# VectorE's preparations for a 3x3 convolution stage move from the attention stage's loop into the convolution stage, whose first band is reordered

## The reference, cut to what matters

```python
q, k, v = to_grid(conv1x1(x, Wq, bq)), to_grid(conv1x1(x, Wk, bk)), to_grid(conv1x1(x, Wv, bv))  # 8x8 pixel windows
attn = softmax(einsum('bgck,bgcl->bgkl', q, k) / sqrt(C))
x = x + from_grid(einsum('bgkl,bgcl->bgck', attn, v))
x = x + conv1x1(gelu(conv1x1(x, W1, b1)), W2, b2)
```

```python
enh = conv3x3_depthwise(conv1x1(x, w_conv1_pw, b_conv1_pw), w_conv1_dw, b_conv1_dw)
h1, h2 = split(conv3x3_grouped(x, w_conv2_g, b_conv2_g))
attn = conv1x1(h1 * h2, w_conv2_pw) * attgamma + conv1x1(x, w_conv211)      # 16 coefficients for each pixel
attk = einsum('bpn,nm->bpm', attn, selfw)                                   # kernels: 2 inputs x 9 taps for each output
x2 = einsum('bpgij,bpgj->bpgi', attk, patches(enh)) + einsum('bpn,nc->bpc', attn, selfb)
x = x2 * ga1 + enh + x
```

## Time and profile before

| | before |
|---|---|
| median of 3 runs | 5592.44 us (5592.13 to 5592.62) |
| the profiled execution | 5592.69 us, its span 5591.0 us |
| TensorE (PE) busy | 5429.2 us, 97% of the span |
| VectorE (DVE) busy | 5155.3 us, 92% |
| GpSimd (POOL) busy | 4484.5 us, 80% |
| ScalarE (ACT) busy | 3471.9 us, 62% |
| mean granted clock of TensorE | 0.994 of full speed |

### The profile page before, as it was taken

The page is one execution under the profiler, slowest core; times in us unless marked ns, Lnnn a source line. Parts: engine busy times, 40 slices in busy tenths (PEclk is TensorE's granted clock), DMA queues, the critical chain, the costliest instruction groups (busy, mean ns, idle before and its releaser), DMA issues.

```text
span 5591.0 us, 112546 instructions
## 1 busy us (share of the span) xinstructions
PE 5429.2 (97%) x37896; PEld 3904.3 (70%) x37896; DVE 5155.3 (92%) x5413; ACT 3471.9 (62%) x4284; POOL 4484.5 (80%) x1959
## 2 busy tenths in 40 slices
PE   8999999999999699999999999999999999999998
PEld 7888888888887366666666666666666666666666
DVE  7888888888888499999999999999999999999999
ACT  6888888888887455555555555555555555555553
POOL 4555555666555699999999999999999999999996
PEclk9999999999999799999999999999999999999999
DMA  2222222222221122222222222222222222222221
GB/s 89 75 75 75 75 75 75 71 72 75 75 75 64 56 71 73 65 77 62 69 73 68 72 69 74 64 77 63 69 73 68 72 68 75 63 77 64 68 74 44
DMA packets 155248, 394.18 MB, mean 71 GB/s; under 512 B 35137, under 2 KB 38401, under 8 KB 155137
## 3 DMA queue, kind: packets, MB, share of 16 engines
q1 hardware_dynamic: 155200, 393.56, 22.6%
HBM read 219.37 MB, written 136.31 MB: 64 GB/s over the span
## 4 chain that ended last, share of the span: by engine, by line
PE 45%; DVE 16%; issue 4%; DVEq 1%; POOL 0%; SPq 0%; ACT 0%; DMA 0%; POOLq 0%
PE ps_k L981 18%; PE ps_t L998 12%; DVE products L1165 11%; PE ps_m L964 8%; DVE products L1171 3%; PE ps_p L951 3%; PE ps_t L1006 2%; PE ps_t L1015 1%; DVE ps_k L1165 1%; PE ps_t L1013 1%; DVE h_prod L1185 1%; POOL enh L917 0%; DVEq L119 0%; SPq L870 0%; DVEq L1169 0%
## 5 line engine op out<-in xcount | busy, mean ns | idle before, releaser
L917 POOL TENSOR_TENSOR enh<-enh,tap 128x1280 f32<-128x1280 f32 (+1 forms) x1024 | 2514.5, 2456 | 224.8 <-ACT tap L1114 178.5
L1165 DVE TENSOR_TENSOR products<-ps_k,enh 128x1024 f32<-128x1024 f32 x1664 | 2001.0, 1218 | 76.2 <-PE ps_k L981 50.0
L981 PE MATMUL ps_k<-att,basis 128*128 128x512 f32 x4608 | 1730.4, 461 | 88.6 <-DVE products L1171 43.6
L981 PEld LDWEIGHTS ps_k<-att,basis 128*128 128x128 f32 x4608 | 719.7, 189 | 870.9 <-DVE products L1165 528.1
L476 POOL TENSOR_TENSOR hidden_lo<-hidden,hidden_hi 128x1024 fp32r<-128x1024 f32 x256 | 694.9, 2735 | 730.2 <-DVE hidden_hi L687 730.2
L1114 ACT ACTIVATE tap<-e,dw 128x1280 f32<-128x1280 f32 (+1 forms) x1024 | 1253.4, 1249 | 4.4 <-POOL enh L917 4.4
L923 POOL TENSOR_TENSOR products<-products 128x1024 f32<-128x1024 f32 x384 | 920.1, 2396 | 74.3 <-DVE products L1165 74.3
L1165 DVE TENSOR_TENSOR ps_k<-ps_k,enh 128x1024 f32<-128x1024 f32 x640 | 784.0, 1225 | 31.8 <-PE ps_k L981 30.8
L1171 DVE TENSOR_TENSOR products<-ps_k,products 128x1024 f32<-128x1024 f32 x640 | 783.5, 1224 | 22.0
L998 PE MATMUL ps_t<-ident_swap,products 128*128 128x128 f32 x5120 | 768.6, 273 | 0.0
L998 PE MATMUL ps_t<-ident,products 128*128 128x128 f32 x5120 | 766.9, 272 | 0.0
(11 more groups left out here) (117 smaller groups left out, 7360.3 us busy)
## 6 DMA issues: line engine op xcount, KB each, us to landing
xin<-layer_out SPq DMA_DIRECT2D x64, 1280.0 KB, 7.2
xt<-in_x SPq DMA_DIRECT2D x128, 512.0 KB, 4.0
layer_out<-xo SPq DMA_DIRECT2D x128, 512.0 KB, 2.9
x_own<-layer_out SPq DMA_DIRECT2D x128, 512.0 KB, 3.8
out<-out_sb SPq DMA_DIRECT2D x256, 256.0 KB, 2.0
att<-att_hi SPq DMA_DIRECT2D x512, 32.0 KB, 2.0
att<-att_lo SPq DMA_DIRECT2D x512, 32.0 KB, 2.0
h_up<-h_sb SPq DMA_DIRECT2D x256, 16.0 KB
```

Of the source, the lines that this page charges most:

```text
L917: nc.gpsimd.tensor_tensor(own, own, tap_sb[add % TAP_BUFFERS][:, 0:hi - lo, :], ALU.add).then_inc(dw_done, 1)
L981: mm = nc.tensor.matmul(ps_k[KERNEL_BUFFER[q]][:, BANK * s:BANK * (s + 1)], basis[:, 2 * t + s, :], att[p][:, j, :], start=True, stop=True)
L1165: nc.vector.tensor_tensor(out, kernels, enh[p][:, r:r + CHUNK_ROWS, dx:dx + W].unsqueeze(1).to_broadcast([C, 2, CHUNK_ROWS, W]), ALU.mult) ...
```

## The change

All of VectorE's preparations leave the attention stage. `make_columns`, `make_grouped`, `make_basis` and `split_basis` now stand one behind another at the head of VectorE's stream in `convolve`, and with them the transpose of the 1x1 weights, for which TensorE has its own first matmul there, into `ps_m`. The DMAs stay in the attention stage; those of `load_pointwise` move from the program's start to the step of tile 1, in front of `load_shared`. `basis_full`, a scratch tensor, now lies in the memory of `products`; `sw_raw` is kept over both stages.

For band 0 the order changes: TensorE makes all 36 grouped taps directly behind the 1x1 convolution, and the coefficients of band 0 stand ahead of band 1's 1x1 convolution. ScalarE does `h_rows` behind tap 5 of the first half and `att_high` behind tap 6, where both stood later. All other bands keep their order.

```diff
-        prepared.place_scratch(sb("sw_raw", [C, 2 * TAPS * C]), sb("basis_full", [C, prepared.SLOTS, C]))
...
-                prepared.load_pointwise(sp)
...
                     if isinstance(l, int) and l == 1:
+                        prepared.load_pointwise(sp)
                         prepared.load_shared(sp)
...
-                pe.wait_ge(wt_ready, 6)
-                pe.wait_ge(prepared.loaded["pointwise"], 16 * prepared.LOADS["pointwise"])
-                nc.tensor.matmul(ring[1][:, 0:C], prepared.pw_raw[:, :], ident[:, :], is_transpose=True,
-                                 start=True, stop=True).then_inc(wt_done, 1)
-                pe.wait_ge(wt_ready, 8)
+                pe.wait_ge(wt_ready, 7)
...
-                dve.wait_ge(wt_done, 8)
-                nc.vector.tensor_copy(prepared.pwT[:, :], ring[1][:, 0:C]).then_inc(wt_ready, 1)
...
-                    if isinstance(l, int) and l == 6:
-                        prepared.make_columns(dve)
-                    if isinstance(l, int) and l == 7:
-                        prepared.make_grouped(dve)
-                    if l is None and m is not None:
-                        prepared.make_basis(dve)
-                    if l is None and m is None and n is not None:
-                        prepared.split_basis(dve)
...
+        ring_memory = products[:, :, :, :].rearrange("c a s n -> c (a s n)")
+        prepared.place_scratch(ring_memory[:, 0:SLOTS * C].rearrange("c (s n) -> c s n", n=C))
...
             def _(pe):
+                pe.wait_ge(prepared.loaded["pointwise"], 16 * prepared.LOADS["pointwise"])
+                pe.wait_ge(prepared.ident_ready, 1)
+                nc.tensor.matmul(ps_m[:, 0:C], prepared.pw_raw[:, :], ident[:, :], is_transpose=True,
+                                 start=True, stop=True).then_inc(prepared.pwT_done, 1)
+                pe.wait_ge(prepared.pwT_ready, 1)
                 pe.wait_ge(swap_ready, 2)
-                pe.wait_ge(grouped_ready, 1)
...
+                            pe.wait_ge(grouped_ready, 1)
...
                         for c in range(PW_CHUNKS):
                             pointwise(l, p, c)
+                        group_taps(l, p, 0, TAPS * CHUNKS)
+                        return
+                    first = isinstance(m, int) and m == 0
+                    if first:
+                        coefficients(m)
...
-                                if band is not None and place == slot:
+                                if band is not None and place == slot and not (first and band is m):
...
-                        if m is not None and at == COEFFICIENT_SLOT:
+                        if m is not None and at == COEFFICIENT_SLOT and not first:
...
-                        if items[k] is not None:
+                        if items[k] is not None and not (first and k == 1 and action in (h_rows, att_high)):
...
+                            if first and k == 1 and action is tap_product and args == (0, 5):
+                                h_rows(items[1])
+                            if first and k == 1 and action is tap_product and args == (0, 6):
+                                att_high(items[1], (p + 1) % 2)
...
             def _(dve):
+                dve.wait_ge(prepared.pwT_done, 1)
+                nc.vector.tensor_copy(pwT[:, :], ps_m[:, 0:C]).then_inc(prepared.pwT_ready, 1)
+                prepared.make_columns(dve)
+                prepared.make_grouped(dve)
+                prepared.make_basis(dve)
+                prepared.split_basis(dve)
                 for p in range(2):
                     nc.vector.memset(att[p][:, :, :].bitcast(FP32), 1.0)
```

8 lines of the change are left out of this document (5 added, 3 removed).

## The result

| | before | after |
|---|---|---|
| median | 5592.76 us (5591.57 to 5593.66, 8 runs) | 5575.41 us (5572.87 to 5576.97, 8 runs) |
| profiled execution, span | 5592.69, 5591.0 us | 5573.84, 5572.1 us |
| mean granted clock | 0.994 | 0.996 |

A forecast was written before the change was run, and what follows sets the result against it. Settled bands, VectorE busy 55.4 and GpSimd 53.5 of 57.1 us, stay untouched; gains come where engines wait in turn. 2.1 + 0.4 + 12.9 + 2.8 = 18.2 us off 5592.7 gives 5574.5, range 5567 to 5583.

The forecast's parts named there:

- Program start: Start of the program: weight and first-tile splits no longer wait for the 1x1 weights' transpose and DMAs; 2.1 us gained.
- Tiles 6 and 7: Attention stage: without the small operations on VectorE, TensorE's 0.43 us wait for hidden_lo goes; 0.4 us gained.
- Drain: End of the attention stage: hidden_hi's halves no longer wait behind basis and split; 12.9 us gained, ends 9.5 and 14.5.
- The rival that the drain gives back half: Drain: GpSimd's subtractions uncovered and TensorE's lower clock leave 6.5 instead of 12.9 us; 5581 to 5584, chance 0.12.
- Start of the convolution stage: Behind the barrier: transpose, copy and four small operations delay the first 1x1 matmul and all hanging on it by 1.4 us.
- The split beside GpSimd: Convolution stage's start: VectorE's split overlaps GpSimd's first additions and holds GpSimd up; 0.8 us lost.
- First band: Band 0 of the convolution stage: 3.6 us from the earlier first product less 0.8 for the split, 2.8 gained.
- The chain named as deciding: Band 0: clearing, ScalarE's chunk copies, TensorE's grouped matmuls, then the first product at 1918.7 us, 3.6 earlier.
- The rival of turns on the shared memory path: First band: GpSimd pays all the split's overlap, ScalarE delivers a tap late; gains nothing to loses 2; chance 0.20.
- The first band didn't gain more: Rival for the first band: band 1's chunks flow faster with att_hi out of ScalarE's way; 5568 to 5570, chance 0.08.
- A worse phase of GpSimd: Rival for the settled bands: GpSimd, starting band 1 later against VectorE, never catches up; 5605 us, chance 0.04.
- The signs: Trace marks: right, barrier 14 to 16 us earlier, first product some 46 behind it; wrong, an addition over 3 us.

The follow-up runs named there:

- small_in_tiles: The changed kernel with make_columns and make_grouped back in the steps of tiles 6 and 7, the transpose left at the head of the convolution stage: 5575.63 us.
- small_at_end: The changed kernel with 1x1-weight transpose, bias columns and grouped weights behind the attention stage's last tile: 5571.98 us, on another chip 5570.29 us.
- basis_only: The kernel before the change with only the basis and its split moved to the head of the convolution stage: 5581.43 us.
- in_gaps: The changed kernel with all preparations but half of the split put where VectorE was idle in the last drain steps: 5574.18 us.
- no_split: The changed kernel with the split of the basis cut to one slot of 19: 5572.94 us.
- reorder_only: The kernel before the change with only band 0 reordered, every preparation left in the attention stage: 5586.42 us.
- no_reorder: The changed kernel with band 0 in its old order, preparations still at the head of the convolution stage: 5580.47 us.
- split_late: The changed kernel with split_basis behind the two fills of att instead of ahead of them: 5576.72 us.

## Why the prediction was right, and where its terms were off

It forecast 5574.5 us in a range of 5567 to 5583 and was 0.9 us low of the median. The size and the place of the largest term, the drain, were right, and that carried the forecast. That it came within a microsecond is luck: by the traces the stretch up to the drain gained 1.6 us more than forecast, the drain 0.4 less and the first band 2.0 less.

- **Program start**, 2.1 taken: 2.13 measured. The four DMA issues moved in SyncE's queue cost nothing that shows.
- **Tiles 6 and 7**, 0.4 taken, ends 0 and 2: `small_in_tiles` shows 1.2 us. The step that failed was to take the one wait of 0.43 us as the price. The small operations hold VectorE for 2.4 us (1853.34 to 1855.78 in `small_at_end`), and half of that counted, almost three times the wait that the row names. Over all, drains of kernels with both edits begin 3.7 us earlier on average (1806.4 in eight profiled executions against 1810.1 in three without them), against the 2.5 predicted. Program start and tiles make 3.3 of it; the other 0.4 is less than the spread between executions.
- **Drain**, 12.9 taken (6.3 in its first step): 12.5 (6.5) by the two attends, 13.8 at the barrier of `basis_only` less the 0.9 by which its drain began earlier (1809.81). The step that used the last drain step's 7.4 us as a model for the others was right, also in that the second cast would be slow: 2.52 and 2.61 us where the row gave 2.31. The rival that the drain gives back half is excluded.
- **Start of the convolution stage**, 1.4 taken, ends 0.7 and 2.5: the first 1x1 matmul was 1.42 later, as forecast. The step that failed was "all that hangs on the 1x1 convolution moves by it": the additions moved by 2.35. The other 0.9 us is TensorE's clock. The window view shows it at the lower of its two levels (1.2 GHz, 0.50) until about 1862.7 in the changed kernel, and only up to 1876.3 in the kernel before, that is 5.2 us against 3.6 from the first matmul on (columns as in the earlier trace rows, for TensorE alone). The wait for VectorE ahead of that matmul doesn't explain it: `in_gaps`, with no such wait, shows 3.62 us for the same group too, and `small_in_tiles`, with a wait of 0.38, shows 2.46. What decides when the clock rises was not tried.

```profile
1859.30:1861.10 1.80, 1.80 (x4) 0.50 1.03 296
1861.10:1862.70 1.60, 1.60 (x3) 0.50 0.64 180
```

```profile
1874.50:1876.30 1.80, 1.80 (x4) 0.52 0.92 302
1876.30:1878.00 1.70, 1.70 (x6) 1.00 1.02 292
```

- **The split beside GpSimd**, 0.8 taken, ends 0 and 5.4: 2.5 us in the series, 2.3 of it at the first product and 2.0 at band 1, by `no_split`. This was the term most under-priced. The working doesn't hold together there: its own times put 3.6 us of the split beside the additions, yet 0.8 was taken, "since about half of the second operation overlaps". That leaves most of the overlap unpaid without a reason. The runs show that the GpSimd addition stops outright. In the changed kernel the overlap was 1871.02 - 1868.38 = 2.64 us and the addition grew by 5.20 - 2.67 = 2.53. The Trainium skill's GPSIMD Engine Reference, section Key points, names VectorE instructions with two SBUF inputs, or in a two-port mode, as contending with GpSimd; how much of an overlap is then paid it doesn't say there. The traces agree: the split and the basis's multiplications in `in_gaps`, each with two, contended, and the fill, with none, did not. For the split they show the overlap paid in full.
- **First band**, 2.8 taken, ends -3 and 5: 0.8. The chain named as deciding was the right one. From the clearing's end to the last grouped matmul it takes 9.6 us (10.4 forecast), the first product follows 0.8 behind. But the clearing came 4.8 us later behind the barrier rather than 1.4, and the product gained only 1.5. And of that 1.5 half is lost at the merges. "0.6 us is left of 5.6" pointed to this, though it compared the merge with the wrong transposes (see `reorder_only`). The series starts 2.35 and ends 4.9 us later. TensorE waits 1.49 us for the first merge and uses it 61.3 us behind the barrier, against 62.9 before; it waits 1.32 for the second and uses it at 66.3, against 67.0.
- **The rival of turns on the shared memory path** gave 5577.5 to 5580 at a chance of 0.20. Its main part was there in full, GpSimd paid all of the overlap, and the first band gained 0.8 where it said "nothing". Its other part, a tap late from ScalarE, was not. Its time was missed mainly since the stretch up to the drain gained 1.6 more than the prediction had. So the forecast's time was met with a first band more like the rival's than its own.
- The fear that ScalarE would be held at `att_hi` did not count: it waited 4.92 us there, for the coefficients, but GpSimd had its taps and the series stayed unbroken. `h_prod` waited for its DMA, not for VectorE's own fills.
- **The other rivals.** The first band didn't gain more. A worse phase of GpSimd didn't come: a settled band takes 57.1 us as before.
- **The signs.** One of those named for "wrong" did come, an addition of over 3 us (5.20). The barrier was 16.65 us earlier where "14 to 16" stood, and the first product 48.3 us behind it where "some 46" stood. The others came as named for "right". The sign of the slow addition told of the term that was in fact off.

## What to carry to other kernels

When setup work is moved out of a latency-bound stretch, look at who is busy where it lands, on every engine: here moving 12 us of VectorE's work gained 12.5 in the drain and cost about 5 in the next stage, which a reordering worth as much gave back. Without it the change still gains (12.9 us in `no_reorder`), but a quarter of the gain goes. A gap of VectorE is free only if what stands in it doesn't meet GpSimd's work and nothing urgent stands behind it. Operations with two SBUF inputs stopped GpSimd one for one or were stopped by it, and the casts of `hidden_hi` waited as well. The fills were seen to pass beside it, and so were the products of PSUM and SBUF (1.23 us at 1924.86 in the kernel before, beside an addition of 2.69). Before speeding up one chain into a join, work out the room to the next one, with each operation set against the one that truly uses it (here 5.55 us, at the second merge): it is the cap of the gain.

## What the runs showed of the hardware

- An elementwise fp32 addition on GpSimd (128x1280, 2.67 us alone) and a subtraction on VectorE with two SBUF inputs (32x2432 on only 32 partitions, 2.68 us alone) did not share the time but took turns: 5.20 and 2.68 in one execution, 2.71 and 5.24 in the next of the same kernel. That a VectorE operation over a quarter of the partitions stops GpSimd completely was unexpected.
- The operation that started first went first: VectorE's by 0.05 us in one execution, GpSimd's by 0.02 in the other. Since both start within a few hundredths of each other, the same program can show either. In `split_late` they alternated (additions of 2.74, 4.93 and 4.95 us, split operations of 3.83 and 5.06), and both lost: 4.6 us on GpSimd and 3.5 on VectorE.
- The attention stage of kernels with the same code up to the drain came to it up to 1.8 us apart from one execution to the next; so the differences of profiled executions in one stage were read from that stage's own start, and those below 2 us over the whole kernel only from medians. A stretch of eight tiles early in the stage, in contrast, agreed within 0.06 us between kernels with the same code there, which is why the 1.2 us of tiles 6 and 7 can be read at all.
